# GRU inputs read back from the output tensor and transposed by VectorE; the output product moved to the bank of V, its copy and its residual to ScalarE and GpSimd

## What is computed

```python
# block 1: attention, within each of the 128 sequences (32 x 32, 16 heads of 16)
scale, shift = split(cond[:, None] @ W_emb + b_emb)
xn = rms_norm(x, g_norm) * (1 + scale) + shift
q, k, v = heads(xn @ W_qkv)
q, k = rms_norm(q, g_q), rms_norm(k, g_k)
o = softmax(q @ k.T * 16 ** -0.5) @ v
x2 = x + o + o @ W_out
# block 2: a GRU over the 32 time steps, h starts as cond
for t in range(32):
    i_r, i_z, i_n = split(x2[:, t] @ W_ih + b_ih)
    h_r, h_z, h_n = split(h @ W_hh + b_hh)
    r, z = sigmoid(i_r + h_r), sigmoid(i_z + h_z)
    n = tanh(i_n + r * h_n)
    h = (1 - z) * n + z * h
    out[:, t] = x2[:, t] + h
```

## Time and profile before

| what | value |
|---|---|
| time of three runs | 342.23, 342.40, 343.04 us; median 342.4 us |
| span of the profiled execution | 340.0 us, the first to the last instruction |
| PE, DVE, ACT, POOL busy | 95%, 72%, 70%, 66% of the span |
| granted TensorE clock | 1.000, in all slices |
| attention, up to the last `residual` | 0 to 190.7 us |
| GRU, from its first product to the end | 191.5 to 340.0 us |

### The profile page before, as it was taken

One profiled execution on the slowest core, in us unless ns is written; L12 is line 12 of the kernel. 1 busy time (PEld: TensorE's weight loads), 2 busy tenths in 40 slices (PEclk: granted clock), 3 DMA queues, 4 the chain that ended last, 5 costly groups with the idle time before them and its releaser, 6 DMA issues.

```text
span 340.0 us, 12168 instructions
## 1 busy us (share of the span) xinstructions
PE 323.3 (95%) x4177; PEld 293.4 (86%) x4177; DVE 246.3 (72%) x665; ACT 238.0 (70%) x722; POOL 224.5 (66%) x404
## 2 busy tenths in 40 slices
PE   8988899899999999999986999999999999999994
PEld 8767788788888888888874999999999999999994
DVE  3778898888999999999996455565555556555555
ACT  4787777778888788889656566666666666666662
POOL 6787787867777877878778346555555555555542
PEclk9999999999999999999999999999999999999999
DMA  5965237742343333233332221111112111122221
GB/s 202 307 193 151 86 76 234 226 132 85 109 121 113 101 114 99 86 117 116 112 109 65 80 77 48 61 49 62 62 62 62 48 58 50 62 62 62 63 62 33
DMA packets 32205, 34.14 MB, mean 100 GB/s; under 512 B 5286, under 2 KB 26796, under 8 KB 32172
## 3 DMA queue, kind: packets, MB, share of 16 engines
q1 hardware_dynamic: 25868, 26.10, 25.6%
q10 hardware_dynamic: 6304, 7.61, 7.0%
HBM read 12.46 MB, written 8.39 MB: 61 GB/s over the span
## 4 chain that ended last, share of the span: by engine, by line
PE 78%; POOL 7%; SPq 4%; DMA 4%; issue 3%; DVE 3%; ACT 1%; POOLq 0%; DVEq 0%; ACTq 0%
PE bank L1287 38%; PE bank L1244 19%; PE bank L1400 4%; PE bank L1419 4%; PE bank L1388 4%; DMA operands<-operands 4%; PE bank L1531 3%; SPq L414 2%; POOL operands L485 2%; PE bank L1380 2%; SPq L405 2%; PE bank L1250 2%; PE bank L1371 2%; POOL xn L496 1%; POOL xn_lo L531 1%
## 5 line engine op out<-in xcount | busy, mean ns | idle before, releaser
L1287 PE MATMUL bank<-wih_lo,wo_parts 128*128 128x256 f32 x192 | 56.2, 294 | 0.0
L1287 PE MATMUL bank<-wih_hi,wo_parts 128*128 128x256 f32 x192 | 54.6, 285 | 0.2 <-POOL pair_lo L600 0.2
L1287 PE MATMUL bank<-wih_hi,pair_lo 128*128 128x256 f32 x192 | 52.8, 279 | 0.0
L1287 PE MATMUL bank<-wqkv_hi,hT_hi 128*128 128x256 f32 x192 | 52.5, 292 | 0.0
L611 POOL TENSOR_TENSOR operands<-operands,h 128x128 f32<-128x128 f32 x64 | 29.6, 462 | 34.2 <-ACT operands L932 33.4
L1287 PE MATMUL bank<-wqkv_lo,hT_hi 128*128 128x256 f32 x192 | 49.9, 279 | 0.0
L1187 DVE TENSOR_TENSOR operands<-bank,operands 128x128 f32<-128x128 f32 x64 | 18.6, 291 | 39.3 <-ACT operands L929 39.3
L1244 PE MATMUL bank<-wqkv_hi,xn_hi 128*128 128x512 f32 (+1 forms) x124 | 46.4, 375 | 0.2 <-POOL xn_lo L531 0.2
L618 POOL TENSOR_TENSOR w_emb_sb<-h,w_emb_sb 128x256 f32<-128x256 f32 x31 | 22.9, 737 | 30.7 <-DVE h L1204 30.7
L1287 PE MATMUL bank<-wqkv_hi,hT_lo 128*128 128x256 f32 x192 | 42.7, 279 | 0.0
L1244 PE MATMUL bank<-wqkv_hi,xn_lo 128*128 128x512 f32 (+1 forms) x124 | 41.9, 338 | 0.0
(11 more groups left out here) (138 smaller groups left out, 975.2 us busy)
## 6 DMA issues: line engine op xcount, KB each, us to landing
v_diag<-v_rows SPq DMA_DIRECT2D x124, 34.0 KB, 2.1
operands<-operands SPq DMA_DIRECT2D x32, 128.0 KB, 2.1
out_dram<-x ACTq DMA_DIRECT2D x16, 256.0 KB, 2.6
w_emb_sb<-out_dram SPq DMA_DIRECT2D x32, 128.0 KB, 2.1
operands<-operands SPq DMA_DIRECT2D x63, 64.0 KB, 2.0
out_dram<-w_emb_sb SPq DMA_DIRECT2D x31, 128.0 KB, 1.7
x_in<-in_x_dram SPq DMA_DIRECT2D x7, 512.0 KB, 8.6
stage_w<-in_L_cond_W_ih_dram ACTq DMA_DIRECT2D x2, 384.0 KB, 3.4
```

The lines of the kernel that those rows point to most:

```text
L1287: return pe.matmul(dst, moved, gate_columns(weights, k, block), start=False, stop=True, skip_group_check=True)
```

## The change

In words:

- **Output product of groups 0 to 22.** PE makes it at lag 11, first in its turn (ahead of V), into the half of bank 1 that shares its bank with V and in which the transposed results stood. ACT copies it to `w_rows`, and POOL adds the input rows, last in its turn (`residual` of POOL), and gives `x2`. It is DVE's work no longer. Groups 23 to 31 go as before, at lag 10.
- **Transposed results.** PE transposes `x2` and ACT copies it out only for groups 24 to 31, and only steps 0 and 1 of it are used. `x2T` is gone.
- **GRU inputs.** SP loads the `x2` of a pair of steps back from the output tensor, in four DMAs, each a quarter (64) of the features, to 32 partitions: partition 32 f + g holds quarter f of group g. DVE transposes the 32 x 32 blocks in one instruction of 128x512. That gives the two steps with features on partitions, features of even and odd number apart, for which W_ih is loaded with its rows in that order. POOL makes the high and low parts from it. For pair 0 that is done for groups 0 to 23 (`early`), in DVE's turn 37, and for groups 24 to 31 as before. Pair 1 is loaded when all of `x2` is stored, and turned by DVE at the start of step 0; the others are turned at the start of every odd step.
- **Stores.** The store of groups 0 to 21 goes one turn later, that of groups 30 and 31 is issued by SP and not by ACT.

The diff, cut:

```diff
+FIRST_TURNED = 24
+NTURNED = NG - FIRST_TURNED
+QF = D // 4
+ADDED = 23
+POOL_ADD, ACT_W, PE_W, ACT_STORE = 11, 11, 11, 12
-        pair_hi = wo_parts
+        pair_hi = sb("pair_hi", [P, 2, 2 * KC, B], F32R)
-        x2T = sb("x2T", [P, KC * T * B])
+        w_rows = sb("w_rows", [P, 2, D])
+        late_x2T = sb("late_x2T", [P, 2 * KC, NTURNED * GB])
+        x_quarters = sb("x_quarters", [P, 2, 2 * D])
+        x_turned = sb("x_turned", [P, 2, 2 * D])
+        def added(o):
+            return o is not None and not (isinstance(o, int) and o >= ADDED)
+        early, late, last_group = slice(0, FIRST_TURNED), slice(FIRST_TURNED * GB, B - GB), slice(B - GB, B)
+        def turned_pair(slot):
+            return x_turned[:, slot, :].rearrange("p (i n g) -> p n g i", i=GB, n=2 * KC)
+        def by_parity(slot):
+            return x_quarters[:, slot, :].rearrange("p (n f c) -> p n c f", n=2 * GB, c=KC)
+        def by_group(pair):
+            return pair.rearrange("p n (g i) -> p n g i", i=GB)
...
# SP, behind its last turn
+            def load_quarters(pair, slot, groups):
+                n = 2 * pair
+                rows = out[groups.start * GB:groups.stop * GB, bass.ds(n, 2), :]
+                for f in range(4):
+                    sp.dma_start(x_quarters[PB * f + groups.start:PB * f + groups.stop, slot, :],
+                                 rows[:, :, f * QF:f * QF + QF]).then_inc(quarters_loaded[slot], 16)
+            early_stores = (NG - FIRST_TURNED) // 4
+            for stored in x2_stored:
+                sp.wait_ge(stored, 16 * (NG // 4 - early_stores))
+            sp.wait_ge(quarters_clear, 1)
+            load_quarters(0, 0, early)
+            sp.wait_ge(x2_ready, summed(NG - 1))
+            sp.dma_start(out.rearrange("(g b) t d -> (b t) g d", b=GB)[:, NG - 2:NG, :], x2[:, 2:4, :])\
+              .then_inc(x2_stored[1], 16)
             for stored in x2_stored:
                 sp.wait_ge(stored, 16 * (NG // 4))
...
+            def next_quarters(pair, slot):
+                sp.wait_ge(quarters_turned, pair - 1)
+                load_quarters(pair, slot, slice(0, NG))
...
+            load_quarters(1, 1, slice(0, NG))
+            load_rows(0, 0)
+            load_rows(1, 1)
+            next_quarters(2, 0)
+            load_rows(2, 2)
+            load_rows(3, 3)
...
# POOL
+            def residual(o, slot, wslot):
+                pool.wait_ge(w_copied, o + 1)
+                if later(o, 4):
+                    pool.wait_ge(x2_stored[slot // 2], (o - slot) * 4)
+                pool.tensor_tensor(x2[:, slot, :], w_rows[:, wslot, :], x_in[:, o, 0:D], ALU.add).then_inc(x2_added, 1)
...
+                o = group(base, u, POOL_ADD)
+                if added(o):
+                    residual(o, (u - POOL_ADD) % 4, (u - POOL_ADD) % 2)
...
+            pool.memset(x_quarters[:, 0, :], 0.0).then_inc(quarters_clear, 1)
...
-            pool.wait_ge(x2T_ready, NG)
+            pool.wait_ge(quarters_turned, 1)
+            pool.tensor_copy(by_group(pair_hi[:, 0, :, :])[:, :, early, :], turned_pair(0)[:, :, early, :])\
+                .then_inc(early_high, 1)
...  (and the low part of the same)
             def high_pair(u, slot):
-                pool.tensor_copy(pair_hi[:, slot, :, :], x2T_pair(u)).then_inc(pair_hi_ready, 1)
+                pool.wait_ge(quarters_turned, u + 1)
+                pool.sem_inc(pair_high_seen, 1)
+                pool.tensor_copy(by_group(pair_hi[:, slot, :, :]), turned_pair(slot)).then_inc(pair_hi_ready, 1)
             def low_pair(u, slot):
-                pool.tensor_tensor(pair_lo[:, slot, :, :], x2T_pair(u), pair_hi[:, slot, :, :].bitcast(F32),
+                pool.tensor_tensor(by_group(pair_lo[:, slot, :, :]), turned_pair(slot),
+                                   by_group(pair_hi[:, slot, :, :].bitcast(F32)),
...
# ACT
+            def output_rows(o, slot):
+                act.wait_ge(w_ps, o + 1)
+                if later(o, 2):
+                    act.wait_ge(x2_added, o - 1)
+                act.copy(w_rows[:, slot, :], p_x2T).then_inc(w_copied, 1)
...
# DVE
                 o = group(base, u, DVE_RES)
-                if o is not None:
+                if o is not None and not added(o):
                     residual(o, (u - DVE_RES) % 4)
...
+                if turn_is(base, u, NG - 1 + DVE_PT):
+                    dve.wait_ge(quarters_loaded[0], 64)
+                    dve.transpose(x_turned[:, 0, :], by_parity(0)).then_inc(quarters_turned, 1)
...
+            def turned_quarters(pair, slot, loads):
+                dve.wait_ge(quarters_loaded[slot], 64 * loads)
+                if later(pair, 3):
+                    dve.wait_ge(pair_lo_ready, pair - 1)
+                dve.transpose(x_turned[:, slot, :], by_parity(slot)).then_inc(quarters_turned, 1)
...
# DVE, in step(base, s), ahead of reset_state(0)
+                if isinstance(t, int) and t == 0:
+                    turned_quarters(1, 1, 1)
+                if s % 2 == 1 and has_pair(base, (s + 3) // 2):
+                    if s == 1:
+                        turned_quarters(pair_index(base, 2), 0, ...)
+                    else:
+                        turned_quarters(pair_index(base, 3), 1, ...)
                 reset_state(0)
...
# PE
+            def output_rows(g, slot):
+                pe.wait_ge(oT_lo_ready, g + 1)
+                pe.wait_ge(v_ready, capped(g, PE_W - PE_V))
+                if later(g, 1):
+                    pe.wait_ge(w_copied, g)
+                output_products(p_x2T, slot).then_inc(w_ps, 1)
...
             def body(base, u):
-                if d is not None and not late_result:
+                if isinstance(d, int) and d >= FIRST_TURNED and not late_result:
                     result_transposes(d, (u - PE_X2T) % 4)
+                g = group(base, u, PE_W)
+                if added(g):
+                    output_rows(g, (u - PE_W) % 2)
...
                 g = group(base, u, PE_OUT)
-                if g is not None:
+                if g is not None and not added(g):
                     output_projection(g, (u - PE_OUT) % 2)
```

More of the change, by code:

```diff
@@ L453, in rows @@
                     load_rows(q * 4 + s + 2, (s + 2) % 4)
-            for t in range(4):
-                load_rows(t, t)
+                if isinstance(q, int) and q == 0 and s == 0:
+                    next_quarters(3, 1)
+                if quarters and s % 2 == 1:
+                    next_quarters(q * 2 + (s + 7) // 2, (s + 7) // 2 % 2)
+            load_quarters(1, 1, slice(0, NG))
[4 more added lines that the diff above has]
+            load_rows(3, 3)
             for s in range(4):
                 rows(0, s)
-            with sp.Fori(1, T // 4 - 1) as q:
+            with sp.Fori(1, T // 4 - 2) as q:
                 for s in range(4):
                     rows(q, s)
+            for s in range(4):
+                rows(T // 4 - 2, s, False)
             for s in range(2):
-                rows(T // 4 - 1, s)
+                rows(T // 4 - 1, s, False)
             store_rows(T - 2, 2)
@@ L1428, in output_projection @@
                 pe.wait_ge(xmod_ready, capped(g, PE_OUT - PE_XT))
-                if isinstance(g, int) and g == 0:
-                    pe.wait_ge(wo_ready, 1)
-                if later(g, 1):
-                    pe.wait_ge(x2_ready, g)
-                products(p_w, [oT_hi[:, slot, c * P:c * P + P] for c in range(KC)],
-                         [oT_lo[:, slot, c * P:c * P + P] for c in range(KC)],
-                         [wo_hi[:, c, :] for c in range(KC)], [wo_lo[:, c, :] for c in range(KC)])\
-                    .then_inc(w_ps, 1)
+                if g > ADDED:
+                    pe.wait_ge(x2_ready, summed(g - 1))
+                output_products(p_w, slot).then_inc(w_ps, 1)
             def body(base, u):
```

108 lines of the change are left out of this document (71 added, 37 removed).

## The result

The changed kernel takes 351.65 us, the median of four runs (350.85 to 353.73); the kernel before, on the same chip, takes 342.31. The ratio is 1.028 [1.0245, 1.0318]: slower by 9.3 us. The forecast was 354.5 in a range of 346.5 to 359.0. Four more runs of the same kernel, made later as an anchor, gave 350.26 (350.01 to 352.57); over all eight the median is 351.0. The profiled execution took 351.18 us, and its span is 349.4, so 1.8 us lie outside.

A forecast was written before the change was run, and what follows sets the result against it. PE was taken to bound the looped turns at 5.05 us, the bound then passing to POOL. Terms -1.0 + 1.4 + 6.7 + 5.0 = +12.1 us, added to 342.4, gave 354.5 us, range 346.5 to 359.

The forecast's parts named there:

- step 0: First GRU step: waits for pair 1's store, loads, transpose and POOL parts ahead of z*h; +6.7 us (+5.2 to +8).
- rival 1: GRU and step 0: POOL's strided read costs nothing, 348.6 us; chance 0.30, with or without the clock.
- phase 1, to turn 33: Attention turns: PE loses transposes, POOL gains the residual; -1.0 us (-4 to +1.5).
- end of attention: DVE's turn 37 waits for four quarter loads and delays group 30; +1.4 us (+0.6 to +2.4).
- clock behind step 0: PE's products behind step 0: no clock cost in the sum; +2.5 to 3.5 us by rival 2.
- rival 2: Step 0: PE idles 7 us and its clock falls, +2.5 to 3.5, 357.5 us; chance 0.20 on top of forecast.
- GRU steps: Later steps: POOL's strided reads lengthen its low part, +0.4 us per two steps, x 13; +5.0 us (0 to 8).
- The bound passes from PE to POOL: Looped turns: POOL's turn becomes 5.00 us, so only 0.05 of PE's 0.22 us is kept.
- Rival 3: Attention turns: PE stays the bound at 4.80 us, 23 turns x 0.27 = 6.2 us gained; chance 0.04.
- The 0.3 us that I took off: Step 0: 0.3 us subtracted since PE has the products of step 1's input done by then.

The follow-up runs named there:

- experiment 4: Changed kernel with POOL reading the turned quarters densely, in the wrong order so that GRU inputs are mixed up: 349.56 us.
- experiment 6: Changed kernel with POOL's residual of groups 0 to 22 adding only 32 of 256 columns: 353.16 us.
- experiment 10: Changed kernel with POOL's residual of groups 0 to 22 going through its columns in strided order, same sums: 361.28 us.
- 5: Changed kernel with DVE's early transpose of pair 0 moved from turn 37 to turn 39, behind group 30's attention-output transpose: 348.55 us.
- Experiment 1: Changed kernel with POOL making pair 1's high and low parts behind z*h and the output row of step 0: 349.01 us.
- experiment 8: Changed kernel with pair 1 also prepared early, both early transposes in turn 39, DVE writing strided, POOL reading dense, pair 2 loaded earlier: 338.45 us.
- experiment 3: Changed kernel with unread products on PE in turns 39 and 40 and step 1, to keep it busy: 350.47 us.
- 7: Changed kernel with DVE writing its transposed blocks strided so that POOL reads each pair densely: 349.24 us.
- 11: The kernel of experiment 8 with DVE's dense write and POOL's strided read, as in the changed kernel: 341.87 us.
- 9: The changed kernel run once more, unaltered, as an anchor: 350.26 us.
- 2: Changed kernel with Experiment 1's order, and DVE turning pair 1 behind step 0 and pair 2 behind step 1: 348.56 us.

## Why the prediction was right, point by point

The direction and its mechanism were right: step 0's round trip to the tensor was forecast as the largest term and was. The forecast was 2.9 us too high against 351.65. That it came so near is luck in part: two terms were 5.6 us too dear together and two 3.3 us too cheap. Nor does the number decide between the forecast and rival 1 (the strided read costs nothing, 348.6), which lies 3.0 us below the measured time; POOL's 1.12 and 1.58 us and experiment 4 do.

| term | predicted | measured | shown by |
|---|---|---|---|
| phase 1, to turn 33 | -1.0 (-4 to +1.5) | -4.0 | 6, 10 |
| end of attention | +1.4 (0.6 to 2.4) | +3.0 | 5 |
| step 0 | +6.7 (5.2 to 8) | +6.4 | 1, 8 |
| clock behind step 0 | 0; by rival 2 +2.5 to 3.5 | +1.7 | 3 |
| GRU steps | +5.0 (0 to 8) | +2.4 | 4, 7, 11 |
| sum | +12.1 | +9.5 | |

**Phase 1 was mis-sized, at the edge of its range of -4 to +1.5.** "The bound passes from PE to POOL" holds, but POOL's turn is 4.84 and not 5.00 us, level with PE's 4.80. The residual takes 0.69 us, as estimated; but POOL's busy time grew by 19.02 / 20 x 4.84 - 15.87 / 20 x 5.05 = 0.60 us a turn, so that by this reckoning it overlaps its neighbours by 0.09 and not 0.03, and the rest of the 0.16 went out of gaps that the waits didn't list (0.29 us of a turn before, 0.24 after; no run takes this apart further). From 83.50 to 151.72, 14 turns, 68.22 us and not 70.69: 2.5 gained, one late DMA included, where I had 0.8 for 16. Ahead of them the gain was 85.56 - 83.50 = 2.1 and not 0.7, though this `shift` stands anywhere from 82.67 to 85.49 in the ten profiles. Turn 33 cost the 0.5 that I gave it: 157.56 - 151.72 = 5.84 us against 5.32. Experiments 6 and 10 close it from both sides: 0.44 us less on POOL is worth 0.04 a turn, 0.51 more costs nearly all of it. Rival 3 put PE's own turn at the 4.80 us that experiment 6 shows, but its 23 turns x 0.27 should be x 0.25 (5.05 - 4.80), 5.8 us.

**The end of attention was mis-sized, above its range of 0.6 to 2.4.** The wait was named in the right place with the right cause: SP's issue, DVE's wait, group 30 behind it. The loads took longer than forecast, 3.40 us and not 2.84 to issue the four, and the last, begun at about 176.79 + 3 x 0.85 = 179.34, had landed at 182.43, 3.1 later and not 2.4. But SP began them earlier, 176.79 - 157.56 = 19.2 us behind the `shift` of turn 33 and not 19.9, so that POOL's low part of group 30 stands 183.99 - 157.56 = 26.4 us behind it, and the forecast had 187.9 - 161.57 = 26.3. What failed is the step from there to R, which was to be as long as before: it takes 5.69 us and not 4.33. The clock, which I had asked about in step 0 alone and which is at 0.50 from 182 to 184 here, makes 1.1 us of that, since the anchor takes 4.59 at full clock. Whether the change brings this fall is open: it isn't in every profile of the changed kernel, and in 13 runs of the kernel before (beside experiments 9 to 11) the mean clock lies between 0.993 and 1.000, so that it isn't always up there either. The anchor's whole term is +2.3 (31.4 against 29.2), inside the range.

**Step 0 was right, nearly part by part**: the transpose at R + 6.7 (forecast R + 7.1), high and low part at 1.06 and 1.51 (1.1 and 1.75), the state at R + 10.83 (R + 11.5). Experiment 1 gives 2.1 us of it to POOL's order, and experiment 8, in which the first pair that needs the round trip is pair 2, takes 6.2 of it away. The 0.3 us that I took off for the products of step 1 that PE has done by then don't show: at full clock the next state comes 4.45 us later (experiment 3) where it was 4.54.

**The clock was rival 2 and came true**, at a smaller price: +1.7 and not 2.5 to 3.5. The sum had it at nothing, with a chance of 0.20 for this rival. PE was idle for 6.26 us, and the clock is back at full in the course of step 1's products: 0.50 in 200 to 204, 0.77 in the next two. The rule of the Trainium skill named in the prediction (TensorE: Matmul & The Clock Gate, The HAM clock gate) had the clock halved here, and the trace agrees.

**The GRU term was mis-sized by half.** The strided read is real: with dense reads the parts fall to 0.61 and 1.31 us and the GRU is 3.0 us shorter. But it isn't one price. The cast became 0.51 us longer for 512 elements, 1.0 ns each; the low part, the one without room, only 0.28, where I had 0.45. PE's waits for `pair_lo` are 12 of together 2.7 us, forecast in the right place. DVE's transpose with its strided input is free, as forecast (0.705 us).

GPSIMD Engine Reference in the Trainium skill (Performance pitfalls for Q7 kernels) gives one extra cycle for each element read with a step over 8 bytes, an estimated 0.43 us here at its 1.2 GHz. The trace agrees for the cast to within 0.1 us, and gives two thirds of it for the low part with one strided operand of two. It exceeds it in experiment 10: with all three operands strided 256 elements cost 0.51 us more, 2.0 ns each.

## What to carry to other kernels

Before you move work off the bounding engine, write down the next engine's turn with its overlaps, not the sum of its instruction times: here the difference between 5.00 and 4.84 us is worth 2.2 us over 14 turns. A transfer that must follow the last store is paid for the greater part wherever the wait for it stands, at DVE, at POOL or at PE: from R to the third new state it takes 13.5 us before, 21.6 in the changed kernel, 19.1 and 18.3 in experiments 1 and 2, which moved the wait, and 14.0 in experiment 8, which took it out of the first steps. So make the data for the first steps by the old road and begin the new one where there are steps to hide it. And where an engine waits some microseconds, look at what PE's clock does next.

## What was unexpected of the hardware

- DVE's transpose of 128x512 in float32 reads with a step at no cost (0.705 us), but writes the blocks with a step at 1.12 us.
- A step on POOL costs 0.51 us on a cast of 512 elements, 0.28 on a two-operand instruction with one strided operand, and 0.51 for 256 elements with all three strided.
- The clock at the end of attention didn't always act alike. In the changed kernel's first profile the granted clock fell to 0.50 there behind idle times of PE of at most 1.53 us; in the anchor's it stayed at 1.00 up to 196 us and fell only in step 0, and in those of experiments 1 and 10 it stayed up there through idle times of 2.24 and 2.12 us. With DVE's wait in place, the way from the last low part to R is 1.1 to 1.3 us longer where it fell. What decides it is open.
